# The attention's score products, each issued a second time into the same banks

## What is computed

```
K_sample = k[:, :, samp_idx, :]
QKs = jnp.einsum('bhle,bhse->bhls', q, K_sample) * scale
M = QKs.max(-1) - QKs.mean(-1)
U = jnp.argmax(M, axis=-1)
q_red = jnp.take_along_axis(q, U[:, :, None, None], axis=2)
scores = jnp.einsum('bhle,bhse->bhls', q_red, k) * scale
attn = jax.nn.softmax(scores, axis=-1)
```

## Time and profile before

| | |
|---|---|
| median of 3 runs | 1283.23 us (1282.82 to 1285.62) |
| profiled execution, its own time | 1285.89 us |
| its span | 1284.0 us |
| mean granted TensorE clock | 0.714 |
| PE busy | 775.3 us (60%) |
| DVE busy | 777.8 us (61%) |
| POOL busy | 593.8 us (46%) |
| the 96 groups of scores | 460.35 to 645.85 us |

### The profile page before, as it was taken

One profiled execution on the slowest core, in us unless ns is written; L12 is line 12 of the kernel. 1 busy time (PEld: TensorE's weight loads), 2 busy tenths in 40 slices (PEclk: granted clock), 3 DMA queues, 4 the chain that ended last, 5 costly groups with the idle time before them and its releaser, 6 DMA issues.

```text
span 1284.0 us, 18781 instructions
## 1 busy us (share of the span) xinstructions
PE 775.3 (60%) x4781; PEld 610.8 (48%) x4782; DVE 777.8 (61%) x2215; ACT 417.0 (32%) x1127; POOL 593.8 (46%) x617
## 2 busy tenths in 40 slices
PE   0106964989998366877677501359999998731000
PEld 0104453779998233443256400238888887621000
DVE  6994366656665458878722699976666665433332
ACT  2464241524444333342001500654545544300000
POOL 8862000255552736552000000357777776377776
PEclk9658965569999556666555655559999999955555
DMA  2390079012222386784400310404434349722222
GB/s 68 127 360 1 1 222 310 1 48 67 71 68 50 85 125 115 121 116 97 48 1 0 94 31 0 136 16 101 105 104 104 105 100 69 78 60 70 61 67 61
DMA packets 116910, 111.06 MB, mean 86 GB/s; under 512 B 16779, under 2 KB 103690, under 8 KB 116618
## 3 DMA queue, kind: packets, MB, share of 16 engines
q1 hardware_dynamic: 101252, 78.56, 24.1%
q0 software_dynamic: 15616, 32.01, 13.5%
HBM read 81.03 MB, written 29.46 MB: 86 GB/s over the span
## 4 chain that ended last, share of the span: by engine, by line
PE 44%; DVE 25%; DMA 10%; POOL 9%; issue 6%; ACT 4%; SPq 2%; DVEq 0%; POOLq 0%; ACTq 0%
PE ps L508 12%; PE ps L502 12%; POOL zbuf L721 8%; DVE zbuf L1058 3%; DMA zbuf<-xrows,holder 3%; DMA big<-parts 3%; DVE bnst L769 3%; DVE zbuf L986 3%; PE ps L1532 2%; PE ps L498 2%; PE ps L1642 2%; PE ps L1560 2%; DMA zbuf<-results,place 2%; PE ps L1683 2%; ACT xbuf L1335 2%
## 5 line engine op out<-in xcount | busy, mean ns | idle before, releaser
L700 POOL DMA_INDIRECT zbuf<-xrows,holder x264 | 254.5, 964 | 139.1 <-PE ps L498 84.8
L721 POOL DMA_INDIRECT zbuf<-results,place x192 | 181.6, 946 | 90.0 <-issue 52.0
L508 PE MATMUL ps<-big,zbuf 128*128 x1328 | 205.0, 286 | 19.5 <-ACT zbuf L470 11.0
L502 PE MATMUL ps<-zbuf,tbuf 128*128 128x128 f32 x1340 | 202.2, 283 | 2.0 <-DVE zbuf L429 2.0
L508 PEld LDWEIGHTS ps<-big,zbuf 128*128 128x128 f32 x1328 | 170.3, 193 | 30.4 <-issue 28.3
L502 PEld LDWEIGHTS ps<-zbuf,tbuf 128*128 128x128 f32 x1340 | 173.9, 195 | 5.7 <-DVE zbuf L429 1.7
L1058 DVE TENSOR_REDUCE zbuf<-ps 125x3 f32<-125x1500 f32 (+1 forms) x96 | 143.1, 1540 | 46.4 <-PE ps L1532 45.6
L470 ACT ACTIVATE zbuf<-ps,tbuf 128x128 f32<-128x128 f32 x335 | 115.2, 366 | 152.7 <-PE ps L502 151.3
L429 DVE COPY zbuf<-ps 128x128 f32<-128x128 f32 x264 | 76.9, 291 | 137.7 <-PE ps L502 133.7
L1532 PE MATMUL ps<-big 97*125 97x500 bf16 x256 | 111.4, 581 | 51.3 <-DVE zbuf L1058 32.2
L1037 DVE SCALAR_TENSOR_TENSOR h<-zbuf,gate,h 125x128 f32<-125x128 f32 x152 | 52.9, 352 | 129.6 <-DMA zbuf<-results,place 128.4
(11 more groups left out here) (352 smaller groups left out, 1166.8 us busy)
## 6 DMA issues: line engine op xcount, KB each, us to landing
results<-zbuf SPq DMA_DIRECT2D x130, 128.0 KB, 1.8
big<-kappa SPq DMA_DIRECT2D x8, 1750.0 KB, 20.8
big<-parts SPq DMA_DIRECT2D x96, 125.0 KB, 6.3
big<-in_L_ffn_W_dram SPq DMA_DIRECT2D x10, 1024.0 KB, 9.2
big<-in_L_ffn_W_dram SPq DMA_DIRECT2D x64, 128.0 KB, 2.7
parts<-zbuf SPq DMA_DIRECT2D x8, 750.0 KB, 4.4
zbuf<-xrows,holder POOLq DMA_INDIRECT x264, 2.6
xrows<-xbuf SPq DMA_DIRECT2D x2, 1792.0 KB
```

Of the source, the lines that this page charges most:

```text
L502: last = t.matmul(ps[:, (2 if k < c.HC // 2 else 4) + u % 2, 128 * k:128 * k + 128], ring.w1[u % U][:, 128 * k:128 * k + 128], ring.rT[u % ...
L508: last = t.matmul(ps[:, 6 + u % 2, 0:D], ring.hid[u % 2][:, 128 * k:128 * k + 128], w2v[:, bass.ds(e, 1), k, :].rearrange("p e d -> p (e d ...
L700: gp.indirect_dma_start(ring.rows[tau % RING], None, xrows[:, :], bass.IndirectOffsetOnAxis(ap=holder[:, tau:tau + 1], axis=0)).then_inc(S ...
L721: gp.indirect_dma_start(got[n % 8], None, results[f][:, :], bass.IndirectOffsetOnAxis(ap=place[f][:, k, t:t + 1], axis=0)).then_inc(S(f"go ...
```

## The change

The loop over the heads of a group is run two times in a row. The second pass has the same operands and the same banks, and it begins a new result (`start=True`), so it writes the numbers of the first again. The semaphore is incremented by the last matmul of the second pass.

```diff
--- before.py
+++ after.py
@@ -1528,7 +1528,7 @@
                     if n >= 2:
                         pe.wait_ge(S("scores_read"), n - 1)
                     j, lo, hi = GROUPS[g]
-                    for head in range(lo, hi):
+                    for head in [*range(lo, hi)] * 2:
                         last = t.matmul(ps[0:R, 3 * (n % 2) + head - lo, 0:L], stack[0:SROWS, 0, b % 2, head, R * j:R * j + R],
                                         stack[0:SROWS, 1, b % 2, head, :], start=True, stop=True)
                     last.then_inc(S("scores_filled"), 1)
```

## The result

The changed kernel takes 1289.49 us (median of 10 runs, 1285.99 to 1293.07) against 1286.25 us (10 runs, 1282.82 to 1287.16) before: ratio 1.0033, 95% interval 1.0020 to 1.0046. It is slower by 3.2 us between the medians and by 4.3 +- 1.6 us between the means, where 1 us faster was forecast. 1289.49 also lies above the range. Part of that distance isn't the change's: the forecast stood on the median of 3 runs, 1283.23, and the median of 10 is 1286.25. Its profiled execution took 1288.88 us (span 1287.2), that of before 1285.89.

The account below looks back on a forecast made before the run. Bound: a chain of waits through the score phases of batches 0, 2, 4, 5 and 7. Terms 1.7 + 1.0 + 1.0 + 0 + 1.7 - 4 x 1.6 - 0.1 = -1.1 us on 1283.23 gave 1282.1 us, range 1279.0 to 1288.5.

Parts of the forecast that it names:

- A high clock makes six matmuls take what three take now: Score rounds: at 2.4 GHz six matmuls take 1.48 us in place of 1.52, a round 4.91 us.
- The 26 us between front4 and the next scores are unchanged: Waits on the chain between score phases, from front4 to the scores two batches later: no scores in them, taken as unchanged.
- From g3's reduction to front4 in 12.1 us: Batches 0, 2, 4 and 5: at the high clock 12.1 us in place of 13.7, a gain of 1.6 each.
- The step that failed: Doubled score rounds: 3.4 us of streaming in 4.91, pauses under a microsecond, so the clock was taken to stay high.
- The fall that I read from the trace of before: Clock fell at about 533.5 us with TensorE busy 0.71 of 2 us; the doubled round was judged nearer the experts loop.
- experts loop: End of the second such loop, 1080 to 1090 us: TensorE busy 6.91 of 10 us, clock 1.00; evidence for a held clock.
- Batch 5 at the high clock, start 0: Start of batch 5: follows batch 4 with hardly a pause, so its clock was taken as high, cost 0.
- The start after a DMA wait, +1.7 or +1.0: Batch starts at the low clock: +1.7 us each in batches 0 and 7, +1.0 each in batches 2 and 4.
- The base: Whole kernel: the sum of -1.1 us was put on the median of 1283.23 us, giving 1282.1.
- Rival B: Scores: the high clock doesn't hold and swings as TensorE waits for VectorE; about +7, 1290 us; chance 0.17.
- Rival C: Scores: the clock never rises and TensorE is the bound in all eight batches; +64, 1347 us; chance 0.03.
- Rival D: Batch starts cost nothing as the clock holds over DMA waits or rises at once; 1279.5 us; chance 0.22.

Follow-up runs that it names:

- e1: The kernel before, unchanged, profiled and timed again on another chip; ratio 1.0015.
- e2: The kernel before with 256 spare matmuls of 500 columns behind the last matmul of TensorE's program; ratio 1.0362 to the kernel before.
- e5: The changed kernel, unedited, once more on another chip; ratio 1.0020 to the kernel before.
- e6: The changed kernel with group g2 of batches 1 to 5 issued five times, not two; ratio 0.9987 to the kernel before.
- e11: The changed kernel with group g2 of batches 1 to 5 issued five times, on another chip than e6; ratio 1.0004 to the kernel before.
- e10: The changed kernel, unedited, a third time, on another chip than e5; ratio 1.0036 to the kernel before.
- e4: The kernel before with the matmuls doubled in batches 6 and 7 only; ratio 1.0027 to the kernel before.
- e9: As e3, plus spare matmuls ahead of batches 0, 2, 4, 6 and 7 during their DMA waits; ratio 0.9991 to the kernel before.
- e3: The changed kernel with group g2 of batches 1 to 5 issued five times, not two; ratio 1.0003 to the kernel before.

## Why the prediction was wrong

The chain of the prediction can be followed phase by phase in the first pair of profiles, from a batch's first score matmul to the end of its front4 (batch 5: from batch 4's front4 to its own; batch 7: to the first matmul of L1548), with the waits between:

| us (rounded) | before | after | forecast change | measured change |
|---|---|---|---|---|
| batch 0 | 20.1 | 20.2 | +0.1 | +0.1 |
| batch 2 | 21.6 | 22.4 | -0.6 | +0.8 |
| batch 4 | 21.6 | 21.7 | -0.6 | +0.1 |
| batch 5 | 23.4 | 21.6 | -1.6 | -1.8 |
| batch 7 | 20.9 | 22.1 | +1.6 | +1.2 |
| the three waits of about 26 | 77.9 | 77.8 | 0 | 0 |
| stretch | 185.5 | 185.8 | -1.1 | +0.3 |

Batches 2 and 4 are what the sum had wrong, by 1.4 and 0.7 us, and in both the clock fell at the pause for the statistics. In batch 2 the start was even cheaper than forecast: it began at the high clock.

Over all profiles the stretch is 185.5, 183.1 and 182.0 us for the single scores (before, e1, e2), mean 183.5, and 185.8, 191.0 and 186.9 us for the doubled ones, mean 187.9. The difference is 4.4 +- 3.8 us, which agrees with the 4.3 +- 1.6 of the timed runs; 3 of the 4.4 lie in the phases and 1.4 in the waits between them, and e5's bad case is in it. That the first pair differed by 0.3 was luck of two single profiles, and so were the 2.3 us ahead of the scores: with identical work ahead of them they scatter over 3.9.

Point by point:

- *A high clock makes six matmuls take what three take now.* Right: 1.50 us a fill, 4.92 us a round.
- *The 26 us between front4 and the next scores are unchanged.* Right in the first pair (table). From the end of front4 to the store of the parts it is 6.7 us in nearly every batch of every profile, single, doubled or three times, so an earlier front4 is passed on whole.
- *From g3's reduction to front4 in 12.1 us.* Right where the clock holds: in batch 0 after, 470.56 to 482.88, 12.3 us, against 13.65 before. Over batches 1 to 5, from g0's reduction to front4 takes 20.0 to 20.5 us before (first profile; 19.7 to 21.0 in e1 and e2), 18.7 with the clock held and 19.7 to 21.2 with a fall. The forecast gain of 1.6 a batch is 1.3 to 1.9 there.
- **The step that failed:** "A round of 4.91 us has 16 x 0.21 = 3.4 us of streaming, in pieces with pauses under a microsecond." That holds for the rounds 2 to 4. In the first round of batches 1 to 5 the statistics stand between two reductions, 1.33 us by the earlier trace rows, and TensorE waits 2.00 us. I had priced them at the batch's start as VectorE's time and not as a pause of TensorE's stream. My own figures give it, for a batch that begins at the high clock as I took batch 5 to do: g0 is filled at 1.48 and read at 3.1, g2's four matmuls end at 3.1 + 1.06 = 4.2, and g3 may be written when the statistics and the reduction of g1 are done, at 3.1 + 1.33 + 1.63 = 6.1. That leaves 1.9 us. The clock fell there in batches 1, 2 and 3 of the profile after and just behind a wait of 1.51 in batch 4, and the twelve matmuls of the next round took up to 5.26 us in place of 2.75. From g0's reduction to front4 a fall costs 19.75 - 18.67 = 1.1 us where it is short and up to 21.2 - 18.7 = 2.5 us where it is long, more than the 1.6 that the high clock was to give: batches 1, 2 and 3 came out 0.4 to 0.8 us slower than before. Filling the pause takes 5.6 +- 2.8 (e6) and 3.3 +- 2.2 us (e11) off the whole time.
- *The fall that I read from the trace of before.* "It fell at about 533.5" is right, but I took its busy share, 0.71 of 2 us, and set it against the 6.91 of 10 us of the experts loop. The fall stands in the very pause that I left out, that of the statistics in batch 3:

```profile
532.85 0.64 PE L1532 MATMUL ps<-big 97*125 97x500 bf16 x2 [0.78 <-DVE zbuf L1058]
535.91 2.76 PE L1532 MATMUL ps<-big 97*125 97x500 bf16 x6 [2.42 <-DVE zbuf L1058]
```

  The experts loop has no wait above 0.61 us between 1080 and 1090, so it could not speak for such a pause.
- *Batch 5 at the high clock, start 0.* Right in the profile after, by luck: its wait of 2.00 us is the one of eleven without a fall. In e5 and e10 the clock fell there.
- *The start after a DMA wait, +1.7 or +1.0.* The mechanism is right and the size too narrow. Batch 7's start cost 1.2 in the profile after (22.1 against 20.9) and 2.0 in e4, e5 and e10 (22.9); where the rise came late, as in batch 4 of e5 (13.7 us), nearly two rounds ran at the low clock. e9 took 3.0 +- 2.4 us off by keeping the clock up over most of these waits.
- *The base.* 1282.1 was 1283.23 less 1.1. On the median of 10 runs the same sum gives 1285.1, and the 1289.49 is 4.3 us above that. So 3.0 of the 7.4 us between forecast and measurement are the scatter of three runs.
- *Rival B.* Its outcome came true, slower because the clock swings, and its place was wrong. It named the rounds in which TensorE waits for VectorE in general; in those without the statistics the clock held, rounds at 4.92 us from 632 to 648. The falls are in one pause per batch. Its price of +7 was about twice the measured one, since only the round after the pause is slow. The Trainium skill, "TensorE: Matmul & The Clock Gate", section "A second HAM failure mode: psum-queue depth-cycling", to whose outcome I gave a chance of 0.17, describes short idle times between groups of matmuls that make the clock swing. The trace shows a swing at the pause of 2.00 us, once a batch, and none at those of 0.54 to 0.57 us between the other groups.
- *Rival C* was refuted: 412 ns a matmul, and the clock mostly high. *Rival D* needed spare matmuls (e9) to come near, and then gave 1 to 2 us (0.9991), within the interval.

The sum with the pauses filled, against before: e3, e6 and e11 are at 0.9987 to 1.0004, about nothing; that agrees with the forecast -1.1 and can't be told from 0. The pauses add the rest. The scatter of the doubled kernel between profiles (185.8 to 191.0) is mostly the clock's: the three waits sum to 77.8, 78.0 and 77.1 us in after, e5 and e10, the five phases to 108.0, 113.0 and 109.8. What sets the moment of a rise, or lets one pause of 2.00 us pass, was not found out.

## What to carry to other kernels

Doubling matmuls in front of a slower engine was nearly free where it lifted TensorE's clock, but the clock has to be followed through every pause of the stream: look for the longest wait in each repetition, not for the mean busy share. Read a fall of the clock by the wait it stands in, and ask where the changed kernel has such a wait. When a low-clock fill is on the path, fill the one long pause with spare matmuls and measure; more passes everywhere cost when a fill gets longer than the reduction beside it (two passes 1.50 against 1.63 us here; three passes cost 26 us). And two profiles of one kernel differed by more in this stretch than the change that was forecast (2.4 against 1.1 us); the timed runs decide, and a profile says only where.

## What the runs showed of the hardware

With the same matmuls the clock rose 3.7 us into one batch (batch 0 after) and 13.7 us into another (batch 4 of e5, with one pause of 0.70 us in it). A wait of 2.00 us between g2 and g3 had a fall in it or within 1.6 us behind it ten times out of eleven (after, e5, e10), while waits of 0.54 to 0.57 us in each round left the clock up for 20 us (batch 6 after, 604.1 to 624.9). And TensorE can stand idle with nothing in the trace to wait for: 30.55 us beside the gathers of e1, and 1.5 to 2.9 us seven times between spare matmuls of e2 (from 1342.06 to 1358.86), most of them after the last gather had started at 1342.07. With no instruction of another engine waiting for them, these spare matmuls set the end of the kernel.
